# Order of work inside a round of a routed two-layer block: centring, roots and gathers laid anew

## The chip, the cores and the metric

The kernel runs on one core of a Trainium2 chip. The metric is the device time of one execution in microseconds; a few executions are timed and the median is given. One further execution is recorded by the hardware profiler, with a time of its own. Engines are called PE (TensorE), DVE (VectorE), ACT (ScalarE), POOL (GpSimd) and SP (SyncE). All times below are microseconds unless they are marked otherwise.

## What is computed

There are 32 samples `x` of 64 rows by 256 columns, eight experts, and an index that names an expert for each sample. Cut to what matters:

```python
h = gelu(einsum('bsh,bhi->bsi', x, Wi[idx]) + bi[idx])   # 256 -> 1024
o = einsum('bsi,bih->bsh', h, Wo[idx]) + bo[idx]         # 1024 -> 256
r = o + x
mu, var = mean(r), mean((r - mu) ** 2)                   # along the 256 columns
y = (r - mu) * rsqrt(var + 1e-12) * gamma[idx] + beta[idx]
```

Everything is fp32. The products are made of three products of rounded parts: each operand is split in a high part (a copy in a rounded format) and a low part (what the copy lost).

## The kernel before, in words

**Blocks.** The samples are sorted by expert on the chip and packed in blocks of four samples (256 tokens) with one expert each. There are at least nine blocks (MIN_BLOCKS), and nine with this data: the profile counts 18 residuals, two to a block. A block's tokens form two tiles of 128, so a block has 2 tiles of output. Work is laid out in rounds, one block a round, and every engine has its own written order; there is no scheduler. Semaphores carry the data dependences between engines, and each engine works strictly in its order.

**PE.** `iteration(t)` (line 862) interleaves four banks of the first product of block t (`first_product`, line 801) with four parts of the second product of block t-1 (`second_product`, line 830): bank 0, part 0, bank 1, part 1 and so on. Each of the eight pieces is 12 matmuls of 128x256. Parts 0 and 1 make tile 0, parts 2 and 3 tile 1. Part 0 waits for the first two pieces of h_lo and the first half of wo's low part, part 1 for pieces three and four and the second half (lines 840 to 849). A bank waits for x_ready, wi_lo and for its bank of `preact` to be free, which the subtraction of h_low frees.

**ACT** (lines 449 to 595) makes high parts: `wi_high` (two halves), `x_high`, `wo_high` (two halves), per bank `gelu` (two activations in place in PSUM) and `h_high`. `deviations(t, tile)` squares r minus its mean and sums it.

**DVE** (lines 597 to 772) makes the low parts: `wi_low`, `x_low`, `wo_low`, `h_low` by subtraction. `centre(t, tile)` adds the product (from PSUM) and xs, sums, makes the negative mean and then (r - mean) * gamma; `finish(t, tile)` makes y with the rstd. `centre_last` is the form for the very last tile.

**POOL** (lines 369 to 447): `residual(t, tile)` (line 390) adds the output bias to the rows x in `xs`; `root(t, tile)` (line 397) makes var + eps (line 401) and its power of -0.5 (line 404) from the sum of squares; `load_x(t)` (line 256) gathers the rows of block t by two indirect DMAs (line 260). DVE's `centre` waits for `xs_ready` from the residual (line 677), ACT's `deviations` for the mean (line 526), POOL's `root` for the deviation (line 400), and DVE's `finish` for the rstd (line 709).

**SP** (lines 317 to 367) issues the other loads: in `iteration(t, ahead)` wi, xT and wo of block t+2, the stores of y(t-2, tile 1), the parameters of block t+2, and the stores of y(t-1, tile 0), in that order. A store waits for its y.

**The ends.** DVE's and ACT's iteration of the last block (no next one) is reached by a branch at run time, `with_next` (line 293); POOL, PE and SP go to their `end` by `from_block` (line 272).

The order of DVE in a round t from 3 on is: centre(t-2,1), wi_low(t+1,0), h_low(t,0), x_low(t+1), finish(t-2,1), centre(t-1,0), wo_low(t,0), h_low(t,1), wo_low(t,1), h_low(t,2), wi_low(t+1,1), h_low(t,3), finish(t-1,0). That of POOL: root(t-2,1), residual(t,0), root(t-1,0), residual(t,1), load_x(t+2), with each residual behind a wait for the wo_low of the same number.

Of the kernel before, what the change touches and what calls it, by code (L numbers as in the profile page):

```python
# [18 lines left out]
def expert_ffn(nc, xr, xt, idx, wi, wo, par, out):  # L19
# [14 lines left out]
    MIN_BLOCKS = E + 1  # L34
# [26 lines left out]
    with ctx:  # L61
# [90 lines left out]
        wo_lo_done = [sem(f"wo_lo_done{i}") for i in range(2)]  # L152
# [103 lines left out]
        def load_x(pool, t):  # L256
            if t >= X_RING:
                pool.wait_ge(stored[t % X_RING], 4 * loads_of(t - X_RING, X_RING))
            for tile in range(2):
                pool.indirect_dma_start(xs[:, t % X_RING, tile, :], None, xr.rearrange("o s h -> (o s) h"),  # L260
                                        rows_of(t, tile)).then_inc(x_loaded[t % X_RING], 16)
# [107 lines left out]
        @block.gpsimd  # L369
        def _(pool):  # L370
            def iota(tile, pattern, base, channel_multiplier=0):
                nc.gpsimd.iota(tile, pattern, base=base, channel_multiplier=channel_multiplier,
                               allow_small_or_imprecise_dtypes=True).then_inc(const_step, 1)

            pool.wait_ge(fills_done, 1)
            nc.gpsimd.affine_select(out=before[:, :], in_=ones[:, 0:B], compare_op=ALU.is_gt, fill=0.0, base=0,
                                    pattern=[[-1, B]], channel_multiplier=1).then_inc(const_step, 1)
            iota(expert_iota[:, :, :], [[1, E], [0, QUAD]], 0)

            iota(sample_less[:, :], [[-1, SLOTS]], -B, 1)  # L380
            iota(place_iota[:, :, :], [[0, E], [1, QUAD]], 0)
            iota(table_base[:, 0:SLOTS], [[1, SLOTS]], B)
            iota(fours[:, :], [[QUAD, MAX_BLOCKS - E]], QUAD)
            iota(slot_iota[:, :], [[1, LATER]], FIRST)
            pool.wait_ge(const_step, 7)
            for half in range(2):

                iota(row_base[half * S:(half + 1) * S, :], [[2 * S, SLOTS // 2]], (B + half) * S, 1)

            def residual(t, tile):  # L390
                if tile == 0:
                    pool.wait_ge(x_loaded[t % X_RING], 2 * loads_of(t, X_RING))
                    pool.wait_ge(par_loaded[t % PAR_RING], loads_of(t, PAR_RING))
                nc.gpsimd.tensor_tensor(xs[:, t % X_RING, tile, :], xs[:, t % X_RING, tile, :], row(0, t),  # L394
                                        ALU.add).then_inc(xs_ready, 1)

            def root(t, tile, last=False):
                at = 2 * t + tile + 1
                if not last:
                    pool.wait_ge(deviation_done, at)  # L400
                    nc.gpsimd.tensor_scalar(var_eps[:, tile:tile + 1], deviation[:, tile:tile + 1], 1.0 / H, LN_EPS,  # L401
                                            ALU.mult, ALU.add).then_inc(var_ready, 1)
                pool.wait_ge(var_ready, at)
                nc.gpsimd.tensor_tensor(rstd[:, tile:tile + 1], var_eps[:, tile:tile + 1], minus_half[:, :],  # L404
                                        ALU.pow).then_inc(rstd_ready, 1)

            def iteration(t, ahead):
                if t == 0:  # L410
                    pool.wait_ge(wo_lo_done[1], 1)
                    residual(0, 0)
                    residual(0, 1)
                elif t == 1:
                    pool.wait_ge(centred_done, 2)
                    residual(1, 0)
                    residual(1, 1)
                    root(0, 0)
                else:
                    root(t - 2, 1)  # L420
                    pool.wait_ge(wo_lo_done[0], t)
                    residual(t, 0)
                    root(t - 1, 0)
                    pool.wait_ge(wo_lo_done[1], t)
                    residual(t, 1)
                if ahead:
                    load_x(pool, t + 2)

            def end(t):

                iteration(t - 2, False)
                iteration(t - 1, False)
                root(t - 2, 1)
                root(t - 1, 0)
                root(t - 1, 1, last=True)

            pool.wait_ge(fills_done, 3)
            pool.wait_ge(table_ready, 1)
            n = entry(pool, T_BLOCKS, MAX_BLOCKS, E)
            pool.wait_ge(rows_ready, 2)  # L440
            load_x(pool, 0)

            pool.wait_ge(wi_loaded[2], 16)
            load_x(pool, 1)
            for t in range(MIN_BLOCKS - 2):
                iteration(t, True)
            from_block(pool, n, MIN_BLOCKS, lambda t, _: iteration(t - 2, True), end)

        @block.scalar
        def _(act):  # L450
# [81 lines left out]
            def iteration(t, has_next):  # L532
                if t == 1:

                    wi_high(2, 0)
                    x_high(2)
                    wi_high(2, 1)
                    wo_high(1, 0)
                    wo_high(1, 1)
                    gelu(1, 0)  # L540
                    h_high(1, 0)
                    gelu(1, 1)
                    h_high(1, 1)
                    gelu(1, 2)
                    h_high(1, 2)
                    deviations(0, 0)
                    deviations(0, 1)
                    gelu(1, 3)
                    h_high(1, 3)
                    return  # L550
                if not has_next:

                    gelu(t, 0)
                    h_high(t, 0)
                    wo_high(t, 0)
                    deviations(t - 2, 1)
                    wo_high(t, 1)
                    gelu(t, 1)
                    h_high(t, 1)
                    gelu(t, 2)  # L560
                    h_high(t, 2)
                    deviations(t - 1, 0)
                    gelu(t, 3)
                    h_high(t, 3)
                    return
                wi_high(t + 1, 0)
                gelu(t, 0)
                h_high(t, 0)
                if t >= 3:
                    deviations(t - 2, 1)  # L570
                x_high(t + 1)
                wo_high(t, 0)
                gelu(t, 1)
                h_high(t, 1)
                wo_high(t, 1)
                deviations(t - 1, 0)
                gelu(t, 2)
                h_high(t, 2)
                wi_high(t + 1, 1)
                gelu(t, 3)  # L580
                h_high(t, 3)

# [15 lines left out]
        def _(dve):  # L598
# [65 lines left out]
            def x_low(t):  # L664
                dve.wait_ge(x_hi_done, t)
                nc.vector.tensor_tensor(x_part(t, 1), x_got(t), x_part(t, 0).bitcast(FP32), ALU.subtract).then_inc(x_ready, 1)
# [46 lines left out]
            def iteration(t, has_next):  # L713
                if t == 1:

                    wi_low(2, 0)
                    x_low(2)
                    wi_low(2, 1)
                    wo_low(1, 0)
                    wo_low(1, 1)  # L720
                    h_low(1, 0)
                    h_low(1, 1)
                    centre(0, 0)
                    centre(0, 1)
                    h_low(1, 2)
                    return
                if not has_next:

                    centre(t - 2, 1)
                    h_low(t, 0)  # L730
                    wo_low(t, 0)
                    finish(t - 2, 1)
                    h_low(t, 1)
                    wo_low(t, 1)
                    centre(t - 1, 0)
                    h_low(t, 2)
                    finish(t - 1, 0)
                    h_low(t, 3)
                    return
                if t == 2:  # L740
                    h_low(1, 3)
                else:
                    centre(t - 2, 1)
                wi_low(t + 1, 0)
                if t == 2:
                    finish(0, 0)
                h_low(t, 0)
                x_low(t + 1)
                finish(t - 2, 1)
                centre(t - 1, 0)  # L750
                wo_low(t, 0)
                h_low(t, 1)
                wo_low(t, 1)
                h_low(t, 2)
                wi_low(t + 1, 1)
                h_low(t, 3)
                finish(t - 1, 0)

            def end(t):
                centre(t - 2, 1)  # L760
# [153 lines left out]
```

## Time and profile before

| | |
|---|---|
| median of 3 executions | 126.82 (126.74 to 126.83) |
| profiled execution, its own time | 125.98 |
| its span, granted clock | 124.2, 0.996 |
| PE busy | 114.4 (92%), 866 matmuls |
| DVE busy | 92.4 (74%) |
| ACT busy | 91.4 (74%) |
| POOL busy | 65.7 (53%) |
| HBM read / written | 27.19 / 2.36 MB, 238 GB/s over the span |

The page's busy figure of PE is an upper one, since the ends of pipelined matmuls are modelled; the distance from start to start tells more. By the page's chain of what ended last, POOL has 43% of the span, DVE 15%, time in which nothing shown was waited for 14%, DMA 9% and PE 9%. This chain goes back from the last instruction to what released each step, and an engine that is always busy beside it does not show in it. In the timelines a bracket at a line's end gives the idle time of the engine before it and what ended it. A round (one block) lasts 11.48. Numbers such as L673 are lines of the kernel.

### The profile page before, as it was taken

The page shows a single profiled execution, that of the slowest core. Times are in us where ns is not written, and L with a number is a line of the kernel's source. Part 1 is how long each engine was busy: PE and PEld are TensorE (multiplying, and loading weights), DVE is VectorE, ACT ScalarE, POOL GpSimd, SP SyncE. Part 2 cuts the span into 40 slices and gives each one's busy share as a digit, 9 for nine tenths or more (in the row PEclk, how much of TensorE's full clock was granted, in tenths as well). Part 3 has the DMA queues.
Part 4 walks back from the last instruction along what each step waited for, and adds up shares of the span by engine and source line. Part 5 has one row for each costly group of instructions (what it writes and reads, how often), then busy time and mean ns, then how long its engine had stood idle before and what let it go on. Part 6 is the DMA issues. An engine that isn't in the chain of part 4 may idle for free.

```text
span 124.2 us, 2707 instructions
## 1 busy us (share of the span) xinstructions
PE 114.4 (92%) x866; PEld 110.7 (89%) x866; DVE 92.4 (74%) x185; ACT 91.4 (74%) x180; POOL 65.7 (53%) x84
## 2 busy tenths in 40 slices
PE   5989999999999989999999999999999999983910
PEld 5878888999999989999999999999999999983900
DVE  3410009989664999799799979997997997698670
ACT  2102479898994998898989889988989875965300
POOL 5033007108984598288819854982798092504420
PEclk9999999999999999999999999999999999999998
DMA  2899999999999914996699589949974200010222
GB/s 73 283 276 300 381 390 407 379 403 380 389 392 383 385 62 111 339 374 235 205 368 387 171 241 384 359 109 314 386 267 113 66 3 26 24 42 0 53 71 66
DMA packets 21399, 29.81 MB, mean 240 GB/s; under 512 B 2368, under 2 KB 11584, under 8 KB 21376
## 3 DMA queue, kind: packets, MB, share of 16 engines
q1 hardware_dynamic: 18464, 23.84, 55.9%
q10 hardware_dynamic: 2048, 3.35, 8.1%
q0 software_dynamic: 864, 2.36, 5.4%
q8 instruction: 9, 0.15, 0.4%
q14 instruction: 14, 0.11, 0.3%
HBM read 27.19 MB, written 2.36 MB: 238 GB/s over the span
## 4 chain that ended last, share of the span: by engine, by line
POOL 43%; DVE 15%; issue 14%; DMA 9%; PE 9%; ACT 4%; SPq 3%; POOLq 0%; DVEq 0%; ACTq 0%
POOL xs L260 15%; POOL xs L394 12%; POOL var_eps L401 8%; POOL rstd L404 7%; PE preact L822 7%; DMA params<-vectors 7%; DVE wo_r L661 6%; DVE r L680 3%; DVE centred L686 2%; DMA xT_in<-x_columns 2%; PE preact L778 2%; SPq L248 2%; DVE xs L710 2%; ACT preact L512 2%; DVE less_mean L683 1%
## 5 line engine op out<-in xcount | busy, mean ns | idle before, releaser
L858 PE MATMUL sums_ps<-wo_r,h_lo 128*128 128x256 f32 x128 | 36.7, 287 | 2.6 <-DVE h_lo L673 2.6
L825 PE MATMUL preact<-xT_r,wi_lo 128*128 128x256 f32 x128 | 36.3, 283 | 0.0
L798 PE MATMUL sums_ps<-wo_r,h_hi 128*128 128x256 f32 x128 | 36.0, 282 | 0.0
L798 PE MATMUL preact<-xT_r,wi_hi 128*128 128x256 f32 x128 | 36.0, 282 | 0.0
L799 PE MATMUL preact<-xT_r,wi_hi 128*128 128x256 f32 x128 | 36.0, 281 | 0.0
L799 PE MATMUL sums_ps<-wo_r,h_hi 128*128 128x256 f32 x128 | 36.0, 281 | 0.0
L260 POOL DMA_INDIRECT xs<-x_rows,row_of x18 | 23.8, 1324 | 18.0 <-DMA wi_in<-w_in 8.5
L394 POOL TENSOR_TENSOR xs<-xs,params 128x256 f32<-128x256 f32 x18 | 18.8, 1050 | 23.0 <-DVE wo_r L661 17.3
L655 DVE TENSOR_TENSOR wi_lo<-wi_in,wi_hi 128x1024 fp32r<-128x1024 f32 x16 | 19.4, 1215 | 11.3 <-ACT wi_hi L481 11.3
L858 PEld LDWEIGHTS sums_ps<-wo_r,h_lo 128*128 128x128 f32 x128 | 24.1, 188 | 3.2 <-DVE h_lo L673 3.2
L825 PEld LDWEIGHTS preact<-xT_r,wi_lo 128*128 128x128 f32 x128 | 24.1, 188 | 0.0
L799 PEld LDWEIGHTS sums_ps<-wo_r,h_hi 128*128 128x128 f32 x128 | 24.1, 188 | 0.0
L799 PEld LDWEIGHTS preact<-xT_r,wi_hi 128*128 128x128 f32 x128 | 24.1, 188 | 0.0
L798 PEld LDWEIGHTS preact<-xT_r,wi_hi 128*128 128x128 f32 x128 | 24.1, 188 | 0.0
L798 PEld LDWEIGHTS sums_ps<-wo_r,h_hi 128*128 128x128 f32 x128 | 24.1, 188 | 0.0
L673 DVE TENSOR_TENSOR h_lo<-preact,h_hi 128x512 fp32r<-128x512 f32 x32 | 21.8, 681 | 2.1 <-ACT h_hi L521 2.1
L512 ACT ACTIVATE preact<-preact,params 128x256 f32<-128x256 f32 x48 | 19.1, 436 | 2.2 <-issue 2.2
L661 DVE TENSOR_TENSOR wo_r<-wo_in,wo_r 128x1024 fp32r<-128x1024 f32 x16 | 20.4, 1278 | 0.3 <-ACT wo_r L496 0.3
L521 ACT ACTIVATE h_hi<-preact 128x512 fp32r<-128x512 f32 x32 | 19.2, 599 | 1.0
L401 POOL TENSOR_SCALAR var_eps<-deviation 128x1 f32<-128x1 f32 x17 | 11.8, 694 | 9.5 <-ACT squares L529 9.4
L481 ACT ACTIVATE wi_hi<-wi_in 128x1024 fp32r<-128x1024 f32 x16 | 16.7, 1051 | 0.0
L496 ACT ACTIVATE wo_r<-wo_in 128x1024 fp32r<-128x1024 f32 x16 | 16.7, 1049 | 0.0
(70 smaller groups left out, 121.4 us busy)
## 6 DMA issues: line engine op xcount, KB each, us to landing
wo_in<-w_out SPq DMA_DIRECT2D x8, 1024.0 KB, 8.4
wi_in<-w_in SPq DMA_DIRECT2D x7, 1024.0 KB, 6.2
params<-vectors SPq DMA_DIRECT2D x9, 388.0 KB, 6.1
y_rows<-xs SPq DMA_DIRECT2D x35, 64.0 KB, 2.1
xT_in<-x_columns SPq DMA_DIRECT2D x34, 64.0 KB, 4.7
wi_in<-w_in ACTq DMA_DIRECT2D x4, 512.0 KB, 5.8
wo_in<-w_out ACTq DMA_DIRECT2D x2, 512.0 KB, 4.6
xs<-x_rows,row_of POOLq DMA_INDIRECT x18, 6.3
```

What stands on the lines that cost most here:

```text
L260: pool.indirect_dma_start(xs[:, t % X_RING, tile, :], None, xr.rearrange("o s h -> (o s) h"), rows_of(t, tile)).then_inc(x_loaded[t % X_RI ...
L394: nc.gpsimd.tensor_tensor(xs[:, t % X_RING, tile, :], xs[:, t % X_RING, tile, :], row(0, t), ALU.add).then_inc(xs_ready, 1)
L401: nc.gpsimd.tensor_scalar(var_eps[:, tile:tile + 1], deviation[:, tile:tile + 1], 1.0 / H, LN_EPS, ALU.mult, ALU.add).then_inc(var_ready, 1)
L512: done = nc.scalar.activation(to, pre, ACT.Gelu, bias=bias[:, c:c + 1])
L521: nc.scalar.activation(h_hi[:, t % 2, 2 * q:2 * q + 2, :].rearrange("p c n -> p (c n)"), preact[:, q, :], ACT.Copy).then_inc(h_hi_done, 1)
L655: nc.vector.tensor_tensor(flat(wi_lo, t % 2, wi_piece(piece)), flat(wi_in, t % WI_RING, wi_piece(piece)), flat(wi_hi, t % 2, wi_piece(piec ...
L661: nc.vector.tensor_tensor(wo_r[:, t % 2, a:b, 1, :], wo_in[:, t % WO_RING, a:b, :], wo_r[:, t % 2, a:b, 0, :].bitcast(FP32), ALU.subtract) ...
L673: nc.vector.tensor_tensor(lo, preact[:, q, :], hi.bitcast(FP32), ALU.subtract).then_inc(h_lo_done, 1)
L798: nc.tensor.matmul(columns, weight, parts[:, 0, :], start=False, stop=False)
L799: return nc.tensor.matmul(columns, weight, parts[:, 1, :], start=False, stop=stop)
L825: nc.tensor.matmul(columns, wi_lo[:, t % 2, c, k, :], xT_r[:, t % 2, k, 0, :], start=(k == 0), stop=False)
L858: nc.tensor.matmul(columns, h_lo[:, t % 2, c, tokens], wo_r[:, t % 2, c, 0, :], start=(c == 0), stop=False)
```

## The change

Data, arithmetic, buffers, PE's order and SP's order stay. POOL's, ACT's and DVE's orders within a round are laid anew:

- POOL's `iteration(t)` now handles residuals of block t-1 and gathers block t+1. In front of the first residual stands a wait for x_ready to reach t+1 (the low part of the next x); root(t-2,1) and root(t-1,0) follow it, then the wait for wo_low(t,1), the second residual and the gathers. Iteration 1 does both residuals of block 0 and root(0,0), then gathers. The last residuals move into `end`.
- ACT: x_high(t+1) moves up behind wi_high(t+1,0); wo_high(t,0) stands in front of deviations(t-2,1). The last block's form becomes the same order without the loads of a next block.
- DVE: x_low(t+1) moves in front of h_low(t,0); wo_low(t,0) in front of centre(t-1,0), and finish(t-2,1) behind it; finish(t-1,0) from the round's end to before wi_low(t+1,1). The last block's form follows.

The diff, cut to its core:

```diff
@@ POOL
             def iteration(t, ahead):
-                if t == 0:
+                if t == 1:
                     pool.wait_ge(wo_lo_done[1], 1)
                     residual(0, 0)
                     residual(0, 1)
-                elif t == 1:
-                    pool.wait_ge(centred_done, 2)
-                    residual(1, 0)
-                    residual(1, 1)
                     root(0, 0)
                 else:
+                    if ahead:
+                        pool.wait_ge(x_ready, t + 1)
+                    residual(t - 1, 0)
                     root(t - 2, 1)
-                    pool.wait_ge(wo_lo_done[0], t)
-                    residual(t, 0)
                     root(t - 1, 0)
-                    pool.wait_ge(wo_lo_done[1], t)
-                    residual(t, 1)
+                    if ahead:
+                        pool.wait_ge(wo_lo_done[1], t)
+                    residual(t - 1, 1)
                 if ahead:
-                    load_x(pool, t + 2)
+                    load_x(pool, t + 1)
             def end(t):
-                iteration(t - 2, False)
                 iteration(t - 1, False)
+                residual(t - 1, 0)
                 root(t - 2, 1)
+                residual(t - 1, 1)
                 root(t - 1, 0)
                 root(t - 1, 1, last=True)
@@ ACT, rounds from 2 on
-                wi_high(t + 1, 0)
+                if has_next:
+                    wi_high(t + 1, 0)
+                    x_high(t + 1)
                 gelu(t, 0)
                 h_high(t, 0)
+                wo_high(t, 0)
                 if t >= 3:
                     deviations(t - 2, 1)
-                x_high(t + 1)
-                wo_high(t, 0)
                 gelu(t, 1)
                 h_high(t, 1)
                 wo_high(t, 1)
                 deviations(t - 1, 0)
                 gelu(t, 2)
                 h_high(t, 2)
-                wi_high(t + 1, 1)
+                if has_next:
+                    wi_high(t + 1, 1)
                 gelu(t, 3)
                 h_high(t, 3)
@@ DVE, rounds from 2 on
                     centre(t - 2, 1)
-                wi_low(t + 1, 0)
+                if has_next:
+                    wi_low(t + 1, 0)
+                    x_low(t + 1)
+                h_low(t, 0)
                 if t == 2:
                     finish(0, 0)
-                h_low(t, 0)
-                x_low(t + 1)
+                wo_low(t, 0)
+                centre(t - 1, 0)
                 finish(t - 2, 1)
-                centre(t - 1, 0)
-                wo_low(t, 0)
                 h_low(t, 1)
                 wo_low(t, 1)
                 h_low(t, 2)
-                wi_low(t + 1, 1)
+                finish(t - 1, 0)
+                if has_next:
+                    wi_low(t + 1, 1)
                 h_low(t, 3)
-                finish(t - 1, 0)
```

The forms for the last block (has_next false) were written out apart before: on ACT gelu and h_high 0, wo_high 0, deviations(t-2,1), wo_high 1, gelu and h_high 1 and 2, deviations(t-1,0), gelu and h_high 3; on DVE centre(t-2,1), h_low 0, wo_low 0, finish(t-2,1), h_low 1, wo_low 1, centre(t-1,0), h_low 2, finish(t-1,0), h_low 3. They are gone.

## Rows read from the trace of the kernel before

**Rows 1.** Windows: stretch, its us; PE, PEld, DVE, ACT, POOL busy; PEclk, DMA share, GB/s.

```profile
45.00:46.00 1.00, 0.67 (x6) 0.46 (x4) 1.00 (x3) 0.97 (x4) 0.94 (x1) 1.00 0.00 0
62.00:73.50 11.50, 11.50 (x99) 11.50 (x98) 10.55 (x20) 10.72 (x22) 7.96 (x8) 1.00 0.86 287
```

**Rows 2.** Timeline of PE over one round; columns start us, duration us.

```profile
58.31 0.28 PE L825 MATMUL preact<-xT_r,wi_lo 128*128 128x256 f32 x1
...
69.02 0.33 PE L858 MATMUL sums_ps<-wo_r,h_lo 128*128 128x256 f32 x1
69.19 0.27 PE L798 MATMUL sums_ps<-wo_r,h_hi 128*128 128x256 f32 x1
...
69.79 0.28 PE L825 MATMUL preact<-xT_r,wi_lo 128*128 128x256 f32 x1
```

**Rows 3.** Timeline of DVE, round t=4 to t=5; idle before and releaser in brackets.

```profile
62.01 0.48 DVE L710 SCALAR_TENSOR_TENSOR xs<-centred,rstd,params 128x256 f32<-128x256 f32 x1 [0.80 <-POOL rstd L404]
...
63.46 1.22 DVE L661 TENSOR_TENSOR wo_r<-wo_in,wo_r 128x1024 fp32r<-128x1024 f32 x1
...
65.20 1.38 DVE L661 TENSOR_TENSOR wo_r<-wo_in,wo_r 128x1024 fp32r<-128x1024 f32 x1
...
68.24 0.68 DVE L673 TENSOR_TENSOR h_lo<-preact,h_hi 128x512 fp32r<-128x512 f32 x1
```

**Rows 4.** Timeline of POOL in the same round.

```profile
64.76 0.74 POOL L394 TENSOR_TENSOR xs<-xs,params 128x256 f32<-128x256 f32 x1 [2.85 <-DVE wo_r L661]
65.47 1.16 POOL L401 TENSOR_SCALAR var_eps<-deviation 128x1 f32<-128x1 f32 x1
66.71 0.55 POOL L404 TENSOR_TENSOR rstd<-var_eps,minus_half 128x1 f32<-128x1 f32 x1
67.23 1.67 POOL L394 TENSOR_TENSOR xs<-xs,params 128x256 f32<-128x256 f32 x1
...
70.52 1.79 POOL L260 DMA_INDIRECT xs<-x_rows,row_of  x1 [0.30 <-issue]
```

**Rows 5.** Waits: engine and line, waited for: us in total, times, longest.

```profile
DVE xs L710 <- POOL rstd L404: 9.2, 11, 1.8
...
PE sums_ps L858 <- DVE h_lo L673: 2.6, 3, 1.2
```

**Rows 6.** Timeline of PE in round t=2.

```profile
45.39 0.28 PE L799 MATMUL sums_ps<-wo_r,h_hi 128*128 128x256 f32 x1
46.01 0.39 PE L858 MATMUL sums_ps<-wo_r,h_lo 128*128 128x256 f32 x1 [0.34 <-DVE h_lo L673]
46.24 0.28 PE L798 MATMUL sums_ps<-wo_r,h_hi 128*128 128x256 f32 x1
```

**Rows 7.** Timeline of PE in the last round.

```profile
111.23 0.28 PE L799 MATMUL sums_ps<-wo_r,h_hi 128*128 128x256 f32 x1
112.71 0.39 PE L858 MATMUL sums_ps<-wo_r,h_lo 128*128 128x256 f32 x1 [1.20 <-DVE h_lo L673]
...
114.71 0.38 PE L858 MATMUL sums_ps<-wo_r,h_lo 128*128 128x256 f32 x1 [1.03 <-DVE h_lo L673]
...
118.25 0.28 PE L799 MATMUL sums_ps<-wo_r,h_hi 128*128 128x256 f32 x1
```

**Rows 8.** Timeline of DVE at the end.

```profile
118.64 0.42 DVE L694 TENSOR_TENSOR r<-sums_ps,xs 128x256 f32<-128x256 f32 x1
```

**Rows 9.** Timeline of ACT at the begin of round t=2.

```profile
32.24 1.05 ACT L481 ACTIVATE wi_hi<-wi_in 128x1024 fp32r<-128x1024 f32 x1
33.19 0.80 ACT L512 ACTIVATE preact<-preact,first_bias 128x256 f32<-128x256 f32 x2
...
34.52 0.62 ACT L488 ACTIVATE xT_r<-xT_in 128x512 fp32r<-128x512 f32 x1
...
35.98 0.80 ACT L512 ACTIVATE preact<-preact,first_bias 128x256 f32<-128x256 f32 x2
```

**Rows 10.** Timeline of ACT at the last round's begin.

```profile
103.95 0.81 ACT L512 ACTIVATE preact<-preact,params 128x256 f32<-128x256 f32 x2 [2.25 <-issue]
```

More of the change, by code:

```diff
@@ L444, in _ @@
             load_x(pool, 1)
-            for t in range(MIN_BLOCKS - 2):
+            for t in range(1, MIN_BLOCKS - 1):
                 iteration(t, True)
-            from_block(pool, n, MIN_BLOCKS, lambda t, _: iteration(t - 2, True), end)
+            from_block(pool, n, MIN_BLOCKS, lambda t, _: iteration(t - 1, True), end)
         @block.scalar
@@ L550, in iteration @@
                     return
-                if not has_next:
-                    gelu(t, 0)
-                    h_high(t, 0)
-                    wo_high(t, 0)
[L556 to L565, printed above, removed]
-                wi_high(t + 1, 0)
+                if has_next:
+                    wi_high(t + 1, 0)
+                    x_high(t + 1)
                 gelu(t, 0)
                 h_high(t, 0)
+                wo_high(t, 0)
                 if t >= 3:
                     deviations(t - 2, 1)
-                x_high(t + 1)
-                wo_high(t, 0)
                 gelu(t, 1)
@@ L726, in iteration @@
                     return
-                if not has_next:
-                    centre(t - 2, 1)
-                    h_low(t, 0)
-                    wo_low(t, 0)
-                    finish(t - 2, 1)
-                    h_low(t, 1)
-                    wo_low(t, 1)
-                    centre(t - 1, 0)
-                    h_low(t, 2)
-                    finish(t - 1, 0)
-                    h_low(t, 3)
-                    return
                 if t == 2:
@@ L743, in iteration @@
                     centre(t - 2, 1)
-                wi_low(t + 1, 0)
+                if has_next:
+                    wi_low(t + 1, 0)
+                    x_low(t + 1)
+                h_low(t, 0)
                 if t == 2:
                     finish(0, 0)
-                h_low(t, 0)
-                x_low(t + 1)
+                wo_low(t, 0)
+                centre(t - 1, 0)
                 finish(t - 2, 1)
-                centre(t - 1, 0)
-                wo_low(t, 0)
                 h_low(t, 1)
@@ L754, in iteration @@
                 h_low(t, 2)
-                wi_low(t + 1, 1)
+                finish(t - 1, 0)
+                if has_next:
+                    wi_low(t + 1, 1)
                 h_low(t, 3)
-                finish(t - 1, 0)
             def end(t):
```

## The prediction

> **What bounds the kernel now.** I read the page's busy times and the waits first, then a round by stretches, then TensorE (PE) matmul by matmul, then the queues of DVE and POOL over one round.
>
> In a whole round PE is busy for all of the 11.50 us at a granted clock of 1.00 (the 2.4 GHz level), while DVE is busy for 10.55, ACT for 10.72 and POOL for 7.96 [rows 1]. A round is 96 matmuls; from one first product's begin to the same point of the next round is 11.48, of which 0.05 is a hitch before one matmul (0.17 from start to start, where 0.12 is the rule) [rows 2]. The matmul there reads the fourth piece of h_lo, and the subtraction that writes that piece (68.24 + 0.68 = 68.92) ends just before it [rows 3]. So PE's own round is 11.43, 0.119 a matmul, and two things bind at once: PE, and a loop without PE in it. I followed that loop through the two queues. DVE's y(t-2,1) waits 0.80 for its rstd; then come the centring of tile 0 and wo_low(t,0); POOL's residual has waited 2.85 for that; behind it stand a root, a residual of 1.67, two gathers (from 68.90 to 72.31), and only then the next rstd that a y waits for [rows 3, 4]. This takes 11.48 too. Without its wait DVE needs 10.6. So DVE and ACT can't catch up with PE, and the lag they start with is carried to the end.
>
> Where the lag costs, PE has three waits on h_lo [rows 5]. In round 2 the fourth piece is late: 0.62 to the next start instead of 0.12, then 0.23: 0.61 lost [rows 6]. In the last round pieces three and four are late: 1.48 instead of 0.12, then 2.00 for six matmuls that are worth 0.72, so 1.36 and 1.28 lost [rows 7], and 0.10 for the slower step behind the last wait, as in rows 6: 2.74. The hitches, one a round over six rounds, are 0.03 to 0.10 each and 0.32 together (rows 2 show one). Sum: **3.67 us** of PE standing behind h_lo.
>
> The end hangs on PE: its last matmul starts at 118.25 and takes 0.28, the last tile's addition starts right behind at 118.64, and the span ends at 124.2 [rows 7, 8]. What PE wins the span wins.
>
> **The change part by part.**
>
> *POOL's queue.* Residuals come one round later (t-1 instead of t), gathers too (t+1 instead of t+2), and both roots stand before the gathers: residual(t-1,0), root(t-2,1), root(t-1,0), residual(t-1,1), gathers. The work is the same 7.96. The 1.67 and the 3.41 of the gathers leave the way to rstd(t-2,1). With every duration at its longest (residual 0.74, two roots of 1.16 + 0.65, where 0.65 is rstd and its hand-over, residual 1.67, gathers 3.41) the queue takes 9.4, under 11.43: it bounds nothing by itself.
>
> *The new wait, x_ready(t+1).* All of POOL's later steps stand behind it, and DVE's centre(t-1,0) waits for the residual. x_low is now DVE's third step; h_low(t,0) and wo_low(t,0) lie between it and the centring, 0.68 + 1.22 less 0.1 of overlap each, 1.7, against 0.8 for the residual. Nothing, with 0.9 of cover; without it each us of delay would stand in DVE's round.
>
> *Blocking between DVE and POOL.* A one-column var_eps begun under wo_low takes 1.16 and ends as wo_low does (66.63 and 66.58); a residual begun under wi_low takes 1.67; a residual and an rstd under h_low, which reads PSUM, take 0.74 and 0.55; the wo_low that begins during a residual takes 1.38, the other 1.22 [rows 3, 4]. So root(t-2,1) may be held to the end of wo_low(t,0) and give its rstd 0.65 later, while its y is wanted one centring (1.05) later: 0 to 0.2 of wait. root(t-1,0) may be held so by wo_low(t,1), with only h_low(t,2), 0.6, before its y: 0 to 0.2. wo_low(t,0) behind the residual: 0 to 0.2. I take 0.3 a round in all, since none of the three has to happen each time, and keep 0 and 0.6. The Trainium skill, page "SBUF — State Buffer", section "SBUF: two separate sides", makes it an exclusive lock between a DVE operation with two SBUF inputs and a GpSimd one that reads SBUF, held for the whole instruction by whoever starts first. That speaks against a residual laid right before a wo_low: by it each round would pay that third wait. The 1.38 beside 1.22 agrees.
>
> *DVE's and ACT's rounds.* The same steps each. DVE: 10.6 + 0.3 = 10.9. ACT: 10.7; its x_high moves up in front of a gelu, which waits for it, 0.5, and its waits for a mean become shorter, since each centring now stands earlier against the square. Both are under 11.43 and gain 0.5 to 0.8 a round on PE until they meet it.
>
> *Round 2 is where the lead comes from.* DVE waits for a rstd eleven times, 9.2 in all; the longest, 1.8, is y(0,1)'s in this round [rows 5]. Now rstd(0,0) comes before the gathers, and y(0,1) stands behind centre(1,0), when its rstd is there. ACT then sets the pace. It starts at 32.24, and its steps are 0.95 (a half of wi or wo), 1.33 (a pair of gelus and h_high), 1.46 (x and a half of wo) [rows 9]: four wide copies and x are 4 x 0.95 + 0.5, four gelu pairs 5.3, one square 0.5, 10.1 in all with its hand-overs. So h_hi(2,3) stands at 42.4 and h_lo(2,3) at 43.1 to 43.3. PE asks for it at 45.5 [rows 6]. The 0.61 goes with 2.2 to spare, and the hitches with it.
>
> *Loads.* SP's loads for t+2 stand behind stores of y's; y(t-1,0) is two DVE steps earlier in its queue now, so they start sooner and are wanted sooner. Round 3 wants wi and x of block 4 at 42.5 to 43.5. Today the DMA engines are idle from 45 to 46 [rows 1], so these had landed by 45: late by 0 to 2. I take 0, as they were issued ahead of other loads; at 2 PE would still get h_lo(3,3) in time (11.43 after 45.5, against 53 to 55). Nothing.
>
> *The last round.* ACT stands 2.25 before gelu(8,0), put down to "issue", and starts at 103.95 [rows 10]. I read it as the jump into the branch without a next block; it stays. Today piece three is asked for at 111.35; two second products of 1.43 lie before that, so the last first product ends at 108.65. With ACT up with PE, the same bank of the round before ends at 108.65 - 11.43 - 0.93 = 96.3 (0.93 is 0.61 + 0.32), gelu(8,0) starts at 96.3 + 1.4 + 2.25 = 100.0, and the last piece goes by PE: bank ready at 107.7, gelus 0.80, h_hi 0.60, h_lo 0.68, hand-overs 0.1, so 109.9. PE asks at 111.35 + 0.72 - 0.93 = 111.1. All 2.74 go, with 1.2 to spare.
>
> **The sum.** 0.61 + 0.32 + 2.74 = 3.67. The profiled execution took 125.98, so 122.3. The median of the runs, 126.82, lies 0.84 above it: 126.82 - 3.67 = 123.15, said as **123.1**. The start and the 5.7 behind PE's end aren't touched.
>
> **Rivals.**
>
> *Half the lead is lost.* The y's waits come at the top of their bounds, or a load holds round 3, or the jump grows, and part of the last two waits stays. For it: two y's hang on roots that a wo_low can hold. Gone are 0.93 and half of 2.74: 2.3, so 124.5. Chance 0.13.
>
> *Nothing comes of it.* The loop closes again at 11.4 to 11.5, through x_low, residual, two roots and y. Against: there are no gathers in that loop. 126.8, chance 0.05.
>
> *Slower.* y(t-1,0) now stands before wi_low(t+1,1) and h_low(t,3), the very piece that PE waits for. If its root is held behind wo_low(t,1), the two y's may wait 0.5 and 0.8 in a round: 10.6 + 1.3 = 11.9, 0.42 over today's 11.48, in rounds 3 to 7: 2.1 more, 128.9. It decides from 0.83 of waits a round (11.43 - 10.6). Against: once the lead is there, that root's square is done some 2 before y's turn. Chance 0.06.
>
> **How the numbers follow.** Full gain 0.76, half 0.13, nothing 0.05, slower 0.06. About 0.2% (0.25 us) is what a measurement can tell from no change. Faster 0.88 (one hundredth of it goes to the slower side for mishaps that I haven't named), same 0.05, slower 0.07. The range reaches 0.5 below the sum, for the run's own offset of 0.84 that may differ, and above past the half case: 122.6 to 124.8.
>
> **What would show it.** Right: no wait of PE on h_lo, rounds of 11.43, last matmul at 114.6, ACT waiting for PE at its gelus in rounds 5 to 7, DVE's waits for a rstd under 0.3 before the end, gelu(8,0) at about 100 behind the same 2.25. Wrong: 0.5 or more of wait before both y's in each round; centre(t-1,0) waiting for its residual; PE waiting for x, wi_lo or a load; waits on h_lo still there in the last round.

## The result, and the profile after

| | before | after |
|---|---|---|
| median of 4 executions | 126.78 (126.20 to 126.83) | 122.34 (121.94 to 122.88) |
| ratio, 95% interval | | 0.9663 (0.9615 to 0.971) |
| profiled execution, span | 125.98, 124.2 | 122.44, 120.7 |
| PE from round 1's first matmul to the last of all | 23.17 to 118.25: 95.08 | 22.99 to 114.51: 91.52 |
| DVE, ACT, POOL busy | 92.4, 91.4, 65.7 | 92.5, 90.8, 54.2 |

The kernel is 3.4% faster, 4.44 us between the medians and 3.54 between the two profiled executions. Here and below the medians are over all executions, and the ratios leave out the slow ones, which lie more than 1.5% above the fastest of their kernel. I had said 123.1, with a range from 122.6: the direction was right, the time 0.8 too high, outside the range. The profiled execution by itself came out as summed (122.3 said, 122.44 measured), so what has to be explained is where the medians win 0.9 more than the profiled pair.

The waits of the kernel after (total us, times, longest); these are its rows that answer to rows 5:

```profile
POOL var_eps L401 <- ACT squares L528: 15.0, 13, 4.2
POOL xs L394 <- DVE xT_r L652: 14.1, 6, 2.5
...
ACT preact L511 <- issue: 2.9, 1, 2.9
...
ACT preact L511 <- PE preact L774: 1.7, 5, 0.5
DVE r L666 <- PE sums_ps L774: 1.6, 3, 1.1
...
DVE xs L696 <- POOL rstd L404: 1.3, 2, 0.8
```

PE's line of waits on h_lo is not there any more. DVE's waits for a rstd have shrunk from 9.2 us in eleven to 1.3 in two, both in DVE's `end`, behind its last h_low. New are ACT's and DVE's waits for PE: they now stand behind it, which is the sign that PE alone binds. ACT's idle time before gelu(8,0) has remained, and is longer.

A round by stretch, as rows 1 (its us; PE, PEld, DVE, ACT, POOL busy; PEclk, DMA share, GB/s):

```profile
62.00:73.50 11.50, 11.50 (x99) 11.50 (x98) 11.36 (x22) 11.15 (x23) 6.44 (x9) 1.00 0.98 319
```

POOL is busy for 6.44 instead of 7.96, and 0.51 of that is a ninth operation, which belongs to the next round: up to 72.90 the eight operations of a round take 5.93. PE's timeline, one first product's begin to the same of the next round, as rows 2:

```profile
68.91 0.28 PE L800 MATMUL preact<-xT_r,wi_lo 128*128 128x256 f32 x1
...
80.35 0.28 PE L800 MATMUL preact<-xT_r,wi_lo 128*128 128x256 f32 x1
```

11.44 from start to start, without a hitch. The end of PE, as rows 7, and the last tile's addition on DVE, as rows 8:

```profile
111.07 0.28 PE L833 MATMUL sums_ps<-wo_r,h_lo 128*128 128x256 f32 x1
...
114.51 0.28 PE L774 MATMUL sums_ps<-wo_r,h_hi 128*128 128x256 f32 x1
```

```profile
109.19 0.69 DVE L659 TENSOR_TENSOR h_lo<-preact,h_hi 128x512 fp32r<-128x512 f32 x1
...
114.90 0.42 DVE L680 TENSOR_TENSOR r<-sums_ps,xs 128x256 f32<-128x256 f32 x1
```

The seventh matmul of that part (111.07) reads the fourth piece of h_lo, finished at 109.88: 1.2 us to spare, where it was 1.3 late. The addition starts 0.39 behind the last matmul, as before.

POOL in the new round, as rows 4:

```profile
62.30 0.73 POOL L394 TENSOR_TENSOR xs<-xs,params 128x256 f32<-128x256 f32 x1 [1.09 <-DVE wo_r L647]
63.19 1.03 POOL L260 DMA_INDIRECT xs<-x_rows,row_of  x1 [0.16 <-issue]
64.52 0.94 POOL L260 DMA_INDIRECT xs<-x_rows,row_of  x1 [0.30 <-issue]
67.92 0.73 POOL L394 TENSOR_TENSOR xs<-xs,params 128x256 f32<-128x256 f32 x1 [2.45 <-DVE xT_r L652]
68.62 1.17 POOL L401 TENSOR_SCALAR var_eps<-deviation 128x1 f32<-128x1 f32 x1
69.87 0.57 POOL L404 TENSOR_TENSOR rstd<-var_eps,minus_half 128x1 f32<-128x1 f32 x1
```

The gathers take 1.03 and 0.94 where they took 1.14 and 1.79, and the residual 0.73 where it took 1.67. The second gather and the residual now begin while DVE is at an h_low (64.37 and 62.13), where they began behind the start of a wi_low (70.27 and 67.10 in the trace of before). The first gather begins 0.05 ahead of a wi_low (63.24) and takes 1.03 beside it; what counts is which of the two began first. The var_eps behind the first residual is still held by wo_low (1.17), as forecast, and nobody waits for it.

### The profile page after: what moved, and what is told of

Same layout as the page of the kernel before. It is cut to its first block, busy times and chain, and to the rows that moved or that the text cites. A ratio compares the mean times of both kernels' runs of the same rounds, so it can differ in the third digit from the quotient of the medians.

```text
span 120.7 us, 2707 instructions
## 1 busy us (share of the span) xinstructions
PE 113.5 (94%) x866; PEld 110.5 (92%) x866; DVE 92.5 (77%) x185; ACT 90.8 (75%) x180; POOL 54.2 (45%) x84
## 4 chain that ended last, share of the span: by engine, by line
PE 92%; issue 2%; POOL 1%; DVE 1%; ACT 0%; DVEq 0%; POOLq 0%
PE preact L800 13%; PE preact L774 13%; PE preact L773 13%; PE sums_ps L833 12%; PE sums_ps L774 12%; PE sums_ps L773 12%; PE preact L797 7%; PE sums_ps L826 6%; PE preact L753 5%; POOL rstd L404 1%; PE sums_ps L768 1%; ACT squares L528 0%; DVE xs L696 0%; DVE r L666 0%; POOL var_eps L401 0%
## 5 line engine op out<-in xcount | busy, mean ns | idle before, releaser
L833 PE MATMUL sums_ps<-wo_r,h_lo 128*128 128x256 f32 x128 | 36.1, 282 | 0.0
L260 POOL DMA_INDIRECT xs<-x_rows,row_of x18 | 18.4, 1025 | 18.1 <-DMA wi_in<-w_in 8.4
L394 POOL TENSOR_TENSOR xs<-xs,params 128x256 f32<-128x256 f32 x18 | 13.4, 747 | 25.2 <-DVE xT_r L652 14.1
L647 DVE TENSOR_TENSOR wo_r<-wo_in,wo_r 128x1024 fp32r<-128x1024 f32 x16 | 19.9, 1250 | 0.4 <-ACT wo_r L495 0.3
L401 POOL TENSOR_SCALAR var_eps<-deviation 128x1 f32<-128x1 f32 x17 | 9.0, 532 | 15.0 <-ACT squares L528 15.0
(70 smaller groups left out, 124.3 us busy)
```

Of the source, the lines that this page charges most:

```text
L647: nc.vector.tensor_tensor(wo_r[:, t % 2, a:b, 1, :], wo_in[:, t % WO_RING, a:b, :], wo_r[:, t % 2, a:b, 0, :].bitcast(FP32), ALU.subtract) ...
L833: nc.tensor.matmul(columns, h_lo[:, t % 2, c, tokens], wo_r[:, t % 2, c, 0, :], start=(c == 0), stop=False)
```

## Experiments

My theory: the gathers and the held residual close a loop of POOL and DVE at 11.48; opened, PE binds at 11.43 and the lead takes the three waits away. The rivals: that the steps of only one of the two sides matter; that the gap of 0.84 is a jump, PE's start, or something in the loop.

**1. The two kernels again, and the jump.** The kernel before unchanged (b_same), the one after unchanged (a_same), and both with ACT's branch to the last block laid the other way round (b_fall, a_fall):

```diff
-            with_next(act, n, MIN_BLOCKS - 1, iteration, end, jump_first=True)
+            with_next(act, n, MIN_BLOCKS - 1, iteration, end)
```

> The kernel before, unchanged, for a second profile. My sum (3.67 less than the profiled 125.98, so 122.3) fits the measured 122.34, and the stated 123.1 missed because 0.84 was added for the gap between profiled execution and median. Theory A: the gap is the idle time of ACT before gelu(8,0), the jump, which was 2.25 in the first profile and 2.93 in the profile after; before the change each us of it comes out at the end. Then this execution's time less 125.98 equals its idle time there less 2.25, within 0.2 us (an idle time of about 3.0 gives 126.7). Theory B: the gap lies elsewhere (start, loads, the store at the end): the idle time stays at 2.25 and the last matmul at another distance.

> The kernel after, unchanged. Theory A: 122.3 again, whatever the idle time before gelu(8,0) is between 2 and 4, since h_lo(8,3) has 1.2 us to spare; no wait of PE on h_lo. Theory B says nothing on it.

> Before, with ACT's branch to the last block laid so that the last block's code comes first and is fallen into, not jumped to. If the 2.25 is the jump and lies on the path, PE's two last waits (1.36 and 1.28) go nearly or all: 2.3 to 2.7 less than before, so 124.1 to 124.6. Rival: the idle time is a wait for something else (parameters of block 8), and nothing moves: 126.8.

> After, with the same edit of ACT's branch. PE is at its floor, so nothing: 122.3, within 0.2. Rival: the jump still costs something at the end, and up to 0.7 goes.

Measured: b_same 127.13 over 12 executions (125.81 to 128.09), the ones of before beside it 126.74 over 23 (125.86 to 127.94). So the first profiled execution, 125.98, was one of the fastest that this kernel has. The profiled one of b_same took 127.18. Its waits of PE in round 2 and in the last round:

```profile
43.12 0.36 PE L858 MATMUL sums_ps<-wo_r,h_lo 128*128 128x256 f32 x1 [0.67 <-DVE wo_r L661]
...
47.27 0.39 PE L858 MATMUL sums_ps<-wo_r,h_lo 128*128 128x256 f32 x1 [0.36 <-DVE h_lo L673]
```

```profile
113.69 0.39 PE L858 MATMUL sums_ps<-wo_r,h_lo 128*128 128x256 f32 x1 [0.87 <-DVE h_lo L673]
...
115.70 0.38 PE L858 MATMUL sums_ps<-wo_r,h_lo 128*128 128x256 f32 x1 [1.03 <-DVE h_lo L673]
```

The two waits of the last round are no longer than in rows 7, so theory A falls: the jump is not where 1.2 us more come from (ACT's idle time before gelu(8,0) is 1.93 there, shorter than the 2.25 of the first trace). New is a wait of PE at 43.12, for wo_low(2,0), where the first trace had a hitch of 0.05. It stands in round 2, behind y(0,1).

a_same took 122.25 over six executions (121.48 to 124.01), as expected; the profiled one was the slowest of them, with round 1 beginning at 24.32 on PE. b_fall took 125.51 (ratio 0.9921, 0.9886 to 0.9955) where 124.1 to 124.6 was expected: the jump does lie on the path of before, and half of the expected gain came. In its trace the last wait of PE is gone and the one before is 0.53 instead of 1.20; from y(0,1) in round 2 to the last matmul it takes 77.4 (39.35 to 116.79), where the kernel before takes 79.1 to 79.4 (section 3 below), so 1.7 to 1.9 are gained. But from the last matmul to the end of the span it takes 7.0 (116.79 to 123.8) instead of 5.95 to 6.4 in the four traces of the kernel before. a_fall pays the same: 123.28, 1 more than a_same, with 115.25 to 122.2 = 6.95 behind its last matmul, where after and a_same have 6.2 and 6.4. Its last store is issued 3.23 behind the last matmul and that of the kernel after 3.24, so the 0.6 to 0.8 lies behind the last store's issue. What it is there isn't shown. The expectation for a_fall missed by that; that PE gains nothing from it (91.5 from first to last) held. In a_fall ACT still stands 1.42 before gelu(8,0), for PE: about half of the 2.93 at that place in the kernel after is time in which PE's bank isn't ready anyway.

**2. The halves of the change alone.** Only the gathers moved, in the kernel before (b_gather):

```diff
                 else:
                     root(t - 2, 1)
+                    if ahead:
+                        load_x(pool, t + 1)
                     pool.wait_ge(wo_lo_done[0], t)
...
-                if ahead:
-                    load_x(pool, t + 2)
+                if t == 0:
+                    load_x(pool, 2)
```

with `end` calling `iteration(t - 2, True)`. Next, DVE's and ACT's new order with POOL's old one (da_only), POOL's new order with the old one of DVE and ACT (pool_only), each made of the whole engine parts of the two kernels, and the kernel after with its gathers put back in front of the roots (a_gfirst):

```diff
                     residual(t - 1, 0)
+                    if ahead:
+                        load_x(pool, t + 1)
                     root(t - 2, 1)
                     root(t - 1, 0)
...
-                if ahead:
+                if t == 1:
                     load_x(pool, t + 1)
```

> Before, with POOL's gathers alone moved: behind root(t-2,1), for block t+1, where POOL idles 2.85 for wo_low, and no other step of any engine moved. My theory: the gathers are what closes the loop at 11.48; without them DVE and ACT gain 0.5 to 0.8 a round and nearly all comes, save part of the 0.61 and more of round 2, whose order stays as it is: 123 to 124. Rival: the steps of DVE and ACT (y three steps behind its centring) make the gain, and this gives less than 1: 126 or more.

> DVE's and ACT's new order with POOL's old one. y(t-2,1) is wanted 2.2 us later in DVE's round, more than its wait of 0.80, so the loop opens also without moving a gather: 122.5 to 124. Rival: old root(t-2,1) still stands behind the gathers and the old residual(t,0) behind wo_low; the waits come back at y(t-1,0), which is wanted earlier: no gain or slower, 126.5 to 128.

> POOL's new order with the old order of DVE and ACT. The root of y(t-2,1) now stands behind x_low(t+1) and a residual, and that y is wanted right behind x_low: it waits 0.8 + 0.2 to 1.2 + 0.65, so 1.7 to 2.6 in each round; DVE's round is 12.3 to 13.2 against 11.48 before: 5 to 10 slower than before, 131 to 137. Rival, by which POOL's order alone frees the roots of the gathers: 122 to 124.

> After, with the gathers put back in front of both roots (behind the first residual). y(t-2,1) is wanted 2.8 behind x_low, its root then comes 0.8 + 2.5 to 3.2 + 0.9 behind it: a wait of 1.4 to 2.1, a round of 12.1 to 12.8, so PE waits 0.6 to 1.3 a round from round 5 on when the lead of 2.2 is used: 125 to 129. Rival: that y has room enough, and the place of the gathers is of no account: 122.3.

| kernel | time | ratio to before, 95% |
|---|---|---|
| b_gather | 122.67 | 0.9632 (0.9532 to 0.9732) |
| da_only | 122.27 | 0.9633 (0.9536 to 0.9731) |
| pool_only | 130.41 | 1.0254 (1.0171 to 1.0338) |
| a_gfirst | 129.85 | 1.0237 (1.0157 to 1.0316) |

Moving two gathers, or moving only DVE's and ACT's steps, each gives what the whole change gives, within the intervals; both came out 0.2 to 0.3 under the times that I had put, 123 and 122.5 at the least. Both open the loop, one by taking 3.4 us out of it, the other by wanting the y 2.2 us later than it was. POOL's new order without DVE's is slower: the y it feeds is wanted right behind x_low, which is where its chain now begins. The y's wait there and in a_gfirst, one row of each for a round:

```profile
63.15 0.48 DVE L709 SCALAR_TENSOR_TENSOR xs<-centred,rstd,params 128x256 f32<-128x256 f32 x1 [1.73 <-POOL rstd L404]
```

```profile
65.30 0.48 DVE L698 SCALAR_TENSOR_TENSOR xs<-centred,rstd,params 128x256 f32<-128x256 f32 x1 [2.10 <-POOL rstd L404]
```

The next such rows are at 75.57 and at 78.19, so the rounds are 12.42 and 12.89: in both the loop binds, not PE. For pool_only I had 12.3 to 13.2 and 131 to 137: the round was right, at its lower end, and the time 0.6 under the range. The loop turns five times, from y(0,1) at 38.17 to the y at 100.4, which is 4.7 more than in the first trace of before. The medians are 3.7 apart: y(0,1) came 0.7 to 2.0 earlier here than in the four traces of the kernel before (38.90 to 40.14). For a_gfirst a wait of 1.4 to 2.1 and 125 to 129 were expected: the wait is at its upper end, and the time 0.85 over the range, since PE waits from round 3 on, not from round 5. The lead of 2.2 that I had counted on wasn't there: the fourth piece of h_lo(2) was ready at 44.60 and read at 44.81, and a round that is 1.45 longer than PE's eats 0.2 at once. So the new order of POOL is worth having only together with that of DVE, and in it the place of the gathers behind the roots decides (7.6 us).

**3. Where the round-2 wait comes from.** SP's load of block 0's parameters moved ahead of wi(3) and xT(3) (b_pearly, a_pearly), and then those of blocks 0 and 1 (b_p01, a_p01); and two more traces of the kernel before (b_rep1, b_rep2).

```diff
             load_wo(sp, 1, 1)
+            load_params(sp, 0, 0)
+            load_params(sp, 1, 1)
             load_wi(sp, 3, 3)
             load_xT(sp, 3)
-            load_params(sp, 0, 0)
             load_wo(sp, 2, 2)
-            for t in range(1, 4):
+            for t in range(2, 4):
                 load_params(sp, t, t)
```

> Before, with the load of block 0's parameters issued ahead of wi(3), xT(3) instead of behind them. Theory C, new: in the kernel before, POOL's first residual waits for these parameters, and the loop of POOL and DVE starts with it, so their landing comes out at the end one for one, less what PE can absorb; two traces of before have it at 27.94 and 29.17 and the last matmul 90.31 and 90.08 behind it. The residual would start at about 26.6 (it also waits for wo_low), so 1.3 to 2.5 earlier than in those two: 124.6 to 125.4 against 126.7. Theory B (the spread comes from PE's start and the end alone): 126.7.

> After, with the same edit of the parameters. Theory C: PE never waits for that loop, so nothing moves: 122.2 within 0.3. If it were faster by 1 or more, the loop would still bind after the change.

> The kernel before once more, for its trace. Theory D, new: in most executions of before, y(0,1) in round 2 is late against PE, since POOL's loop starts with the landing of the parameters, so PE waits there 0.6 us or more for wo_low(2,0), which the first profiled execution (125.98) did not; and the last matmul starts 79.0 to 79.4 after y(0,1), wherever that is. Rival: PE's wait there is an exception, and the distance varies.

> As b_rep1: last matmul 79.0 to 79.4 behind y(0,1); a wait of PE for wo_low(2,0) of 0.6 or more, unless this is again an execution of about 126.0.

> Before, with the parameters of blocks 0 and 1 both issued ahead of wi(3). With block 0's alone POOL's residuals of block 1 waited for theirs until 31.87, and y(0,1) stayed at 38.76. Theory D: now the first residual starts at about 26.6, y(0,1) at 37.3 to 37.8, and the last matmul 79.2 behind it: 116.5 to 117.0, the time 124.3 to 125.3. Rival: y(0,1) hangs on something else, stays at 38.7 or later, and the time at 126.7.

> After, with the same edit. By theory D PE alone sets the end, 91.5 from its first matmul of round 1 to its last, whatever the parameters do; that first matmul may come later, since wi(3) and others stand behind more bytes: 122.2 to 124.1 as with block 0's alone. If the length is under 91.4 or the time under 121.8, something else still bound.

b_pearly missed: 127.26, nothing. Its first residual came at 26.53, but the next ones waited 1.54 for block 1's parameters, until 31.87, and y(0,1) stayed at 38.76. Theory C as I had put it was wrong: not the first landing alone sets the loop. With both early, b_p01's y(0,1) comes at 37.24, in the expected place. Put together, for the kernel before (us from the span's start):

| trace | PE begins round 1 | first residual | y(0,1) | last matmul | y(0,1) to last matmul |
|---|---|---|---|---|---|
| before (125.98) | 23.17 | 27.94 | 38.90 | 118.25 | 79.35 |
| b_same (127.18) | 23.33 | 29.17 | 40.14 | 119.25 | 79.11 |
| b_rep1 (127.11) | 23.31 | 28.72 | 39.69 | 118.86 | 79.17 |
| b_rep2 (127.10) | 23.43 | 29.04 | 40.00 | 119.17 | 79.17 |
| b_p01 (124.31) | 21.43 | 26.23 | 37.24 | 116.36 | 79.12 |
| b_pearly (127.22) | 21.79 | 26.53 | 38.76 | 119.42 | 80.66 |

Over 2.9 us of spread the last matmul keeps its distance of 79.1 to 79.4 to y(0,1); the odd one, b_pearly, lost 1.5 of its 80.66 to a lower clock in the last round (last section). PE's beginning of round 1 varies too, and the last two rows tell the two apart: it is 0.36 apart, y(0,1) 1.52, and the last matmul, with the 1.5 of the clock taken off, 1.56. And in b_pearly PE began 1.4 earlier than in the first trace, and the last matmul, with the 1.5 taken off, came 0.3 earlier. So the end of the kernel before hangs on the loop's start, and not on when PE begins. b_rep1's y, with its usual wait, and PE's wait that follows:

```profile
39.69 0.48 DVE L710 SCALAR_TENSOR_TENSOR xs<-centred,rstd,params 128x256 f32<-128x256 f32 x1 [1.81 <-POOL rstd L404]
```

```profile
42.66 0.36 PE L858 MATMUL sums_ps<-wo_r,h_lo 128*128 128x256 f32 x1 [0.46 <-DVE wo_r L661]
...
46.81 0.39 PE L858 MATMUL sums_ps<-wo_r,h_lo 128*128 128x256 f32 x1 [0.33 <-DVE h_lo L673]
```

PE's waits for wo_low(2,0), from start to start and less 0.12, cost 0.61 in b_rep1, 0.80 in b_rep2, 0.83 in b_same, 0.75 in b_fall, and 0.05 in the trace that I predicted from. b_p01's median is 125.97 over ten (ratio 0.9866, 0.9805 to 0.9927), with executions from 124.31 to 127.65: faster, but above the 124.3 to 125.3 that I expected, which its profiled execution alone met. Where y(0,1) came in the others isn't known.

In the kernel after PE's length doesn't move with any of this: 91.52 (after), 91.52 (a_same, first matmul at 24.32), 91.59 (a_p01, at 23.34), 91.60 (a_pearly, at 24.52). a_p01 took 122.39 (0.9548, 0.9451 to 0.9646), no better than the kernel after. a_pearly missed: 124.03 (122.33 to 124.25) where 122.2 was expected, with a round 1 that began 1.5 late in its trace. That its edit is the reason isn't shown: a_same, without it, began as late, and a_p01, b_p01 and b_pearly, with such an edit, at 23.34, 21.43 and 21.79; and its wi(3) was issued at 18.00, when PE had already begun the second product of block 0 (17.81), the last before round 1. In these traces the time of the kernel after hangs on when PE begins round 1. An earlier beginning than theirs gains less: in a_pad1 below it was 21.48, and PE then stood 1.0 us for h_lo(1,2) and (1,3).

**4. How much lateness the kernel after absorbs.** One and three copies of 128x1024 more on ACT before gelu(8,0), on a tile of their own (a_pad1, a_pad3); POOL fills that tile once, ahead of its second gathers.

```diff
+                else:
+                    act.wait_ge(pad_filled, 1)
+                    for i in range(3):
+                        if i:
+                            act.wait_ge(pad_step, i)
+                        nc.scalar.activation(pad[:, :], pad[:, :], ACT.Copy).then_inc(pad_step, 1)
```

> After, with one copy of 128x1024 more (1.05 us) on ACT before gelu(8,0). The spare that I put at 1.2 for h_lo(8,3) (1.17 by the trace of after, and 0.18 that ACT waits for PE before it) hides it: no wait of PE in the last round, 122.3.

> After, with three such copies (2.9 us back to back) on ACT before gelu(8,0). 1.35 of it is hidden; the rest, 1.5, comes back as a wait of PE for h_lo(8,3) or (8,2) in the last round: 123.8 to 124.2, more where the clock falls behind that wait. If it costs 2.9, there was no spare; if nothing, the end doesn't hang on this chain.

a_pad1 has no wait of PE in the last round. Its median is 123.11 over four executions (121.90 to 123.87), which is above the 122.3 expected; at this spread that tells little, and why isn't settled, and in its trace the only waits of PE are in round 1, where it began at 21.48 and ran ahead of h_lo(1,2) and (1,3). a_pad3 took 124.10. ACT's copies and PE's two waits:

```profile
100.10 3.24 ACT L562 ACTIVATE pad<-pad 128x1024 f32<-128x1024 f32 x3 [2.68 <-issue]
```

```profile
110.98 0.39 PE L843 MATMUL sums_ps<-wo_r,h_lo 128*128 128x256 f32 x1 [0.76 <-DVE h_lo L669]
...
112.38 0.39 PE L843 MATMUL sums_ps<-wo_r,h_lo 128*128 128x256 f32 x1 [0.42 <-DVE h_lo L669]
```

From start to start PE loses 0.92 and 0.58 and 0.10 behind each: 1.7 of the 3.24. The idle time before the copies was 2.68 here and 2.93 in the trace of after, so 3.0 were added, and 1.3 hidden. I had put 1.35.

## Why the prediction was right, and where it failed

**What binds.** Right. The loop through y(t-2,1), centring, wo_low, residual, root, residual, gathers was the second bound: taking the gathers out of it alone gives all of the gain (b_gather), and putting them back into the new order's chain costs 7.6.

**The three waits and the hitches.** Right in the profiled execution: 3.67 said, 95.08 - 91.52 = 3.56 measured between first and last matmul; the last matmul said for 114.6, found at 114.51; the round 11.43 said, 11.44 found. The restart steps, the hitches and the three waits are all gone. That the whole came within 0.15 of 122.3 is in part luck: round 1 began 0.18 earlier than before, and the time behind the last matmul was 0.24 longer (6.19 instead of 5.95), neither by the change.

**Round 2.** Right in its result: h_lo(2,3) is no longer late, and y(0,1) comes at 38.59 with no wait. The lead was smaller than said: h_lo(2,3) was ready at 43.64 (43.1 to 43.3 said) and read at 45.31 (45.5 said), 1.7 and not 2.2.

**The new wait on x_ready, the held roots.** Right in kind. The residual waits for x_low 14.1 us in six, before a centring that doesn't wait for it in these rounds. A var_eps is held for 1.17, and wo_low takes 1.38 behind the residual where the other one takes 1.22. The Trainium skill, page "SBUF — State Buffer", section "SBUF: two separate sides", has a lock between a DVE operation with two SBUF inputs and a GpSimd one that reads SBUF, held for the whole instruction, and these rows agree with it. No y waits for any of this, where I had taken 0.3 a round: DVE's rounds last 10.70 until it meets PE (its y's at 49.30, 60.00 and 70.70), and 10.9 was said. POOL's work was not the same, as I had written: 5.93 a round instead of 7.96, 54.2 instead of 65.7 in all, since part of what the profile calls busy on POOL was being held.

**The last round.** Right in its result, wrong in one term: I kept the jump at 2.25, and it was 2.93. gelu(8,0) came at 100.66, not 100.0, and h_lo(8,3) at 109.88 (109.9 said), since that last piece goes by PE. The spare of 1.2 was there, and a_pad3 shows its size (1.3 hidden).

**The sum.** Here it failed. The step is: "The median of the runs, 126.82, lies 0.84 above it: 126.82 - 3.67". That took the 0.84 for a constant beside the stalls. A good part of it is itself stall: the profiled execution was among the fastest of the kernel before, with PE almost free of waiting for wo_low(2,0) (0.05, one of the hitches in the sum); in four other traces with that order (b_same, b_rep1, b_rep2, b_fall) that wait costs 0.61 to 0.83, and all of it goes with the change, because y(0,1) no longer stands in front of wo_low(2,0) and centre(1,0).

Not all of it adds to the sum, since the end hangs on y(0,1): the first of the last two waits is then shorter, 1.02 to 1.15 instead of 1.36. From the first matmul of round 1 to the last of all PE took 95.92, 95.55 and 95.74 in b_same, b_rep1 and b_rep2, so it loses 4.0 to 4.4 against the 91.52 of the kernel after, where the first trace had 3.56. With these the sum is 126.8 less 4.0 to 4.4, 122.4 to 122.8; 122.34 was measured. The three executions took 1.1 to 1.2 more than the first one: 0.5 to 0.8 of that is stall, and the rest, which the change doesn't touch, is a later beginning of round 1 (0.14 to 0.26) and a longer time behind the last matmul (0.2 to 0.5). No execution at the median itself was traced, so how its 0.84 divides isn't shown. My range also allowed only 0.5 for that offset, while I had the number 0.84 in hand and knew no cause for it.

**The rivals.** None came true. The jump grew, as one had it, and was hidden. The slower one, y's held in front of h_low(t,3), would have taken waits that never came: no y waits in any round, and only two in DVE's `end`.

Why the parameters and gathers of the first blocks land at different times from execution to execution isn't settled. In b_same, b_rep1 and b_rep2 the granted clock is 0.79 on average from 8 to 16 us, where the first trace has 1.00, and the 32 first matmuls take 8.86 instead of 8.25. But they also started earlier: wi(3), which waits for them, was issued only 0.14 to 0.25 later, the parameters 0.14 to 1.07 later, and the first residual came 0.8 to 1.2 later. So part of it is the transfers' own time.

## What to carry to other kernels

When one engine shows no gaps and a chain without it has the same period, both bind; look at the one small hitch a round that tells that they touch, and open the loop at the step that no one needs early. Either side of the loop will do, a producer's long step moved behind its result or the consumer moved later, but half of a joint reordering can cost more than all of it gains. And when a median stands off the profiled execution, ask which wait in the trace is short by luck before carrying the gap over as a constant: a second trace of the kernel before would have shown most of it.

## What the runs showed of the hardware that I had not expected

- PE's standing in the last round can cost a second time. In b_pearly, after waits of 0.94 and 1.04, the granted clock went to the lower level (1.2 GHz) while the last products ran, and 16 matmuls went 0.21 apart instead of 0.12, 1.5 us lost. b_same, with waits of 0.87 and 1.03, kept its clock, so it isn't certain to happen; pool_only fell too. In the kernel after PE doesn't stand there, and the clock stays at 1.00 until its work is done. Windows of b_pearly:

```profile
110.00:114.00 4.00, 2.36 (x18) 1.96 (x17) 3.40 (x8) 1.97 (x6) 1.45 (x3) 1.00 0.13 33
114.00:116.00 2.00, 1.65 (x11) 1.65 (x12) 1.80 (x8) 0.60 (x2) 0.37 (x2) 0.80 0.29 70
116.00:118.00 2.00, 2.00 (x11) 2.00 (x11) 1.18 (x4) 0.60 (x2) 1.16 (x3) 0.50 0.06 12
```

- ACT's idle time at the jump is not a constant: 2.25, 1.93, 2.04 and 2.01 in traces of the kernel before, 2.93 and 2.70 in two of the kernel after, and 2.94 and 2.17 in a_pearly and a_p01.
- Laying ACT's last branch so that it is fallen into takes the jump's idle time away and lengthens the time behind the last matmul, in both kernels: 6.95 and 7.0, against 5.95 to 6.5 in the sixteen traces with the jump.
- In these traces an operation of POOL is long when it begins behind the start of a wi_low or wo_low, and not when it begins just ahead of one: a gather took 1.79 begun 0.25 behind a wi_low, and 1.03 begun 0.05 ahead of one; a var_eps took 1.17 begun 0.27 behind a wo_low, and 0.19 begun clear of one.
